# Expert layers of a macaron block: probability moved into the gated product, rows passed on summed in PSUM, token numbers as bfloat16 parts, scatters and gathers in pairs

## What is computed

```python
scores = softmax(xf @ gate_w.T)                  # 8192 x 64
_, idx = top_k(scores + gate_b, 6)               # six experts of each token
# the first 128 tokens that chose expert e fill its 128 slots, in order; later ones are dropped
h  = silu(xb[e] @ w1[e].T) * (xb[e] @ w3[e].T)   # 128 x 176 for each of 64 experts
yb = h @ w2[e].T                                 # 128 x 256
y[token of slot] += yb * scores[token, e]
z  = silu(xf @ ws1.T) * (xf @ ws3.T) @ ws2.T     # shared expert, all tokens
x  = x + 0.5 * (y + z)
```

## Time and profile before

| | us |
|---|---|
| median of three runs | 1974.1 |
| the profiled execution's own time | 1970.14 |
| its span in the trace | 1968.3 |
| PE busy | 1787.3 (91%) |
| DVE busy | 1337.4 (68%) |
| ACT busy | 1095.1 (56%) |
| POOL busy | 837.4 (43%) |

### The profile page before, as it was taken

The page is one execution under the profiler, slowest core; times in us unless marked ns, Lnnn a source line. Parts: engine busy times, 40 slices in busy tenths (PEclk is TensorE's granted clock), DMA queues, the critical chain, the costliest instruction groups (busy, mean ns, idle before and its releaser), DMA issues. The chain is left out here.

```text
span 1968.3 us, 31892 instructions
## 1 busy us (share of the span) xinstructions
PE 1787.3 (91%) x10553; PEld 1097.5 (56%) x10554; DVE 1337.4 (68%) x3338; ACT 1095.1 (56%) x2260; POOL 837.4 (43%) x923
## 2 busy tenths in 40 slices
PE   5999999899955889999999999999699999989997
PEld 2565656677732345444444444445356666657775
DVE  3787877566637567777777777767168787856664
ACT  3676776111113667777777777777466766731111
POOL 1010100687735665555555555550000111027777
PEclk9999999999978989999999999999899999999999
DMA  2233331799943333333333333332213343339997
GB/s 94 87 99 113 117 119 57 221 261 261 262 78 80 91 82 107 99 98 106 101 98 101 104 99 99 98 87 56 89 48 105 92 138 97 100 93 261 264 263 157
DMA packets 193342, 245.21 MB, mean 125 GB/s; under 512 B 17658, under 2 KB 160410, under 8 KB 193182
## 3 DMA queue, kind: packets, MB, share of 16 engines
q1 hardware_dynamic: 168606, 205.43, 34.4%
q0 software_dynamic: 24576, 37.77, 10.0%
HBM read 127.78 MB, written 63.86 MB: 97 GB/s over the span
## 5 line engine op out<-in xcount | busy, mean ns | idle before, releaser
L1332 DVE TENSOR_REDUCE a_smax<-a_p_ring 128x1 f32<-128x512 f32 (+2 forms) x768 | 353.7, 505 | 151.3 <-PE a_p_ring L1419 146.2
L1237 ACT ACTIVATE a_probs<-a_p_ring 128x512 f32<-128x512 f32 x640 | 363.8, 606 | 105.3 <-PE a_p_ring L1431 104.0
L1419 PE MATMUL a_p_ring<-p_ks,p_qs 100*128 100x512 bf16 (+3 forms) x1024 | 245.2, 304 | 43.1 <-ACT a_probs L1237 20.1
L48 POOL TENSOR_TENSOR f_rstd<-f_mv,eps 128x4 f32<-128x4 f32 x32 | 26.0, 813 | 552.9 <-DVE f_mv L42 548.4
L1431 PE MATMUL a_p_ring<-p_qs,p_ks 103*128 103x512 bf16 (+3 forms) x1024 | 243.2, 304 | 5.8 <-ACT a_probs L1237 5.4
L629 ACT ACTIVATE e_silu<-e_p_up 128x176 f32<-128x176 f32 x128 | 40.7, 318 | 353.6 <-PE e_p_up L719 226.4
L458 PE MATMUL f_p_up<-f_xnT,f_ws1T 128*128 128x512 f32 x384 | 187.9, 612 | 1.5 <-ACT f_xnT L253 1.5
L595 POOL DMA_INDIRECT e_got<-rows,slot_token x128 | 126.4, 988 | 141.5 <-issue 81.5
L499 PE MATMUL f_p_z<-f_ws2T,f_hidden 128*128 128x256 f32 (+1 forms) x768 | 184.5, 391 | 1.9 <-DVE f_hidden L346 1.9
L1447 PE MATMUL a_p_out<-a_probs,p_v 128*32 128x512 f32 (+3 forms) x2048 | 176.8, 445 | 6.2 <-ACT a_probs L1237 6.2
L458 PE MATMUL f_p_up<-f_xnT,f_ws3T 128*128 128x512 f32 x384 | 181.5, 595 | 0.0
(11 more groups left out here) (156 smaller groups left out, 3572.0 us busy)
## 6 DMA issues: line engine op xcount, KB each, us to landing
h_w<-w_in SPq DMA_DIRECT2D x128, 352.0 KB
p_qs<-a_parts SPq DMA_DIRECT2D x192, 128.0 KB, 2.4
p_ks<-a_parts SPq DMA_DIRECT2D x192, 128.0 KB, 2.5
h_w<-w_in SPq DMA_DIRECT2D x128, 176.0 KB
rows<-f_row SPq DMA_DIRECT2D x32, 640.0 KB, 6.3
h_x<-x_in SPq DMA_DIRECT2D x16, 512.0 KB, 6.0
acc<-h_x SPq DMA_DIRECT2D x16, 512.0 KB, 3.1
a_x<-acc SPq DMA_DIRECT2D x16, 512.0 KB, 4.0
```

What stands on the lines that cost most here:

```text
L1237: nc.scalar.activation(to[:], p_score[s][:], ACT.Exp, scale=SCALE).then_inc(score_free[s], 1)
L1332: ins = nc.vector.tensor_reduce(smax[:, t, 4 * g + h:4 * g + h + 1], p_score[s][:, at:at + length], AX.X, ALU.max)
L1419: ins = nc.tensor.matmul(p_score[s][:, at:at + length], qs[1 - u][0:SR + MASK, 4 * g + h, t * P:(t + 1) * P], ks[1 - u][0:SR + MASK, 4 * g ...
```

## The change

- Twelve lanes for the gathered rows instead of eight (`GOT`), with twelve gathers ahead; the lane counts on over both layers.
- On POOL the loop issues scatter e and e + 1, and after every odd one the next two gathers, instead of one gather ahead of each scatter.
- The probability is multiplied in by the instruction that multiplies the two halves on DVE; the factor 0.5 goes into ACT's copy of the turned product.
- The join matmul accumulates into `p_y` behind the w2 product; DVE then only copies `p_y` to `y`, and the second DVE instruction and its bank `p_join` are gone.
- The token numbers are split in two parts that bfloat16 holds exactly (tile times 128, and lane); `spread` does two bfloat16 matmuls for each expert instead of one in float32.
- `table` outlives the routing stage, `place` takes its folded content, and a bfloat16 identity is kept.

```diff
+GOT = 12
-        got = [sb(f"got{s}", [P, ROW]) for s in range(LANES)]
+        got = [sb(f"got{s}", [P, ROW]) for s in range(GOT)]
...
+        def lane(e):
+            return (to.first + e) % GOT
...
-                for e in range(LANES):
+                for e in range(GOT):
                     gather(e)
                 for u in range(XR):
                     pool.wait_ge(to.acc_stored[u], 16 * B // XR)
                 for e in range(E):
-                    pool.wait_ge(y_scaled, e + 1)
-                    if e + LANES < E:
-                        gather(e + LANES)
+                    pool.wait_ge(y_copied, e + 1)
                     wait_count(pool, added[e % 2], 16 * (e // 2))
                     if e % GROUP == 0:
                         pool.wait_ge(redirected, e // GROUP + 1)
                     add(e)
+                    if e % 2:
+                        for n in range(e - 1 + GOT, min(e + 1 + GOT, E)):
+                            gather(n)
...
-                    nc.scalar.copy(hiddenT[e % 2][:], p_hidden[:]).then_inc(hiddenT_ready, 1)
+                    nc.scalar.activation(hiddenT[e % 2][:], p_hidden[:], ACT.Copy, scale=0.5).then_inc(hiddenT_ready, 1)
...
-                    nc.vector.tensor_tensor(hidden[e % 2][:], silu[e % 2][:], p_up[e % 2][:, I:2 * I],
-                                            ALU.mult).then_inc(hidden_ready, 1)
-
-                def scale(e):
+                    nc.vector.scalar_tensor_tensor(hidden[e % 2][:], silu[e % 2][:], got[lane(e)][:, e + D:e + D + 1],
+                                                   p_up[e % 2][:, I:2 * I], ALU.mult,
+                                                   ALU.mult).then_inc(hidden_ready, 1)
+
+                def bring_y(e):
 
                     dve.wait_ge(y_ready, e + 1)
                     wait_count(dve, added[e % 2], 16 * (e // 2 - LANES // 2 + 1))
-                    ins = nc.vector.tensor_scalar(y[e % LANES][:], p_y[e % 2][:], got[e % LANES][:, e + D:e + D + 1],
-                                                  0.5, ALU.mult, ALU.mult)
-                    if e:
-                        dve.drain()
-                        ins = nc.vector.tensor_tensor(y[e % LANES][:], y[e % LANES][:], p_join[:], ALU.add)
-                    ins.then_inc(y_scaled, 1)
+                    nc.vector.tensor_copy(y[e % LANES][:], p_y[e % 2][:]).then_inc(y_copied, 1)
 
                 def tokens():
 
                     nc.vector.tensor_copy(token[:], w.slot_token[:])
+                    nc.vector.tensor_scalar(vacant[:], w.table[:, 1, :], 0.0, None, ALU.is_equal)
+                    nc.vector.tensor_scalar(tile_base[:], w.table[:, 1, :], float(P), float(-P), ALU.mult, ALU.add)
                     dve.drain()
+                    nc.vector.scalar_tensor_tensor(token_lane[:], vacant[:], w.lane[:, 0:1], w.table[:, 0, :],
+                                                   ALU.mult, ALU.add)
+                    nc.vector.scalar_tensor_tensor(token_tile[:], vacant[:], float(DUMMY + P), tile_base[:],
+                                                   ALU.mult, ALU.add)
...
                     for g in range(2):
                         ins = nc.tensor.matmul(p_y[e % 2][:], hiddenT[e % 2][:, g, :], w2[e % slots][:, g, :],
-                                               start=(g == 0), stop=(g == 1))
+                                               start=(g == 0), stop=(g == 1 and e == 0))
 
                     if e:
-                        pe.wait_ge(y_scaled, e)
+                        pe.wait_ge(y_copied, e)
                         if (e - 1) % GROUP == 0:
                             pe.wait_ge(redirected, (e - 1) // GROUP + 1)
-                        ins = nc.tensor.matmul(p_join[:], same[(e - 1) // GROUP % 2][:, (e - 1) % GROUP, :],
-                                               y[(e - 1) % LANES][:], start=True, stop=True)
+                        ins = nc.tensor.matmul(p_y[e % 2][:], same[(e - 1) // GROUP % 2][:, (e - 1) % GROUP, :],
+                                               y[(e - 1) % LANES][:], start=False, stop=True)
...
-                        ins = nc.tensor.matmul(p_tokens[:, k, :], token[:, after:after + 1].to_broadcast([P, P]),
-                                               w.ident[:], start=True, stop=True)
+                        nc.tensor.matmul(p_tokens[:, k, :], token_tile[:, after:after + 1].to_broadcast([P, P]),
+                                         w.ident16[:], start=True, stop=False)
+                        ins = nc.tensor.matmul(p_tokens[:, k, :], token_lane[:, after:after + 1].to_broadcast([P, P]),
+                                               w.ident16[:], start=False, stop=True)
```

More of the change, by code:

```diff
@@ L81, in open_arrivals @@
     arrivals.x_loaded = [ctx.enter_context(nc.semaphore(f"x_loaded{u}")) for u in range(XR)]
-    arrivals.gathered = [ctx.enter_context(nc.semaphore(f"gathered{s}")) for s in range(LANES)]
+    arrivals.gathered = [ctx.enter_context(nc.semaphore(f"gathered{s}")) for s in range(GOT)]
     arrivals.weights_loaded = [ctx.enter_context(nc.semaphore(f"weights_loaded{s}")) for s in range(LANES)]
@@ L90, in open_handover @@
     to.x_loaded, to.x_rounds = arrivals.x_loaded, layer * B // XR
-    to.gathered, to.gather_rounds = arrivals.gathered, layer * E // LANES
-    to.weights_loaded, to.first_load = arrivals.weights_loaded, layer * E
+    to.gathered = arrivals.gathered
+    to.weights_loaded, to.first = arrivals.weights_loaded, layer * E
     to.w13 = [ctx.enter_context(nc.sbuf_tensor(f"{tag}_w13_{s}", [P, DC, SI], F32))[:] for s in range(LANES)]
@@ L162, in route_and_share @@
         hidden = [sb(f"hidden{j}", [P, T]) for j in range(3)]
-        table = sb("table", [P, 2, E])
-        empty = sb("empty", [P, E])
+        table, empty, place = w.table, sb("empty", [P, E]), sb("place", [P, E])
         zero = sb("zero", [P, P], BF16)
@@ L431, in _ @@
                 nc.vector.tensor_scalar(empty[:], table[:, 1, :], 0.0, w.dummy_row[:, 0:1], ALU.is_equal, ALU.mult)
[L432 to L433 removed]
+                nc.vector.scalar_tensor_tensor(place[:], table[:, 1, :], float(P), table[:, 0, :], ALU.mult, ALU.add)
                 dve.drain()
[L435 removed]
+                nc.vector.scalar_tensor_tensor(w.slot_token[:], place[:], float(-P), empty[:],
                                                ALU.add, ALU.add)
@@ L595, in gather @@
                     nc.gpsimd.indirect_dma_start(
-                        out=got[e % LANES][:], out_offset=None, in_=dram.rows,
+                        out=got[lane(e)][:], out_offset=None, in_=dram.rows,
                         in_offset=bass.IndirectOffsetOnAxis(ap=w.slot_token[:, e:e + 1].bitcast(U32), axis=0),
-                    ).then_inc(gathered[e % LANES], 16)
+                    ).then_inc(gathered[lane(e)], 16)
                 def add(e):
@@ L698, in _ @@
                     if e:
-                        scale(e - 1)
+                        bring_y(e - 1)
                     if e % GROUP == 2 and e // GROUP + 1 < E // GROUP:
@@ L707, in turn @@
                 def turn(e):
-                    pe.wait_ge(gathered[e % LANES], 16 * (e // LANES) + 16 * to.gather_rounds + 16)
+                    pe.wait_ge(gathered[lane(e)], 16 * ((to.first + e) // GOT) + 16)
                     wait_count(pe, xT_ready, e)
                     for h in range(DC):
-                        ins = nc.tensor.transpose(p_turn[:, h, :], got[e % LANES][:, h * P:(h + 1) * P], w.ident[:])
+                        ins = nc.tensor.transpose(p_turn[:, h, :], got[lane(e)][:, h * P:(h + 1) * P], w.ident[:])
                     ins.then_inc(turned, 1)
```

15 lines of the change are left out of this document (8 added, 7 removed).

## The result

The changed kernel takes **1984.56 us** in the median of 13 runs (1979.7 to 1991.39), the kernel before in the same session 1974.52 (13 runs, 1971.23 to 1979.39). The ratio is 1.0049, with an interval of 1.0038 to 1.0060: slower by about 10 us, where 7.5 us of gain were forecast. The time lies above the stated range of 1955 to 1978 us, in the direction of the rival "Landings grow: slower".

What follows compares the result with a forecast made beforehand. POOL and the landing of its scatters were taken to set each expert stage's end, PE having slack. Gains of 2.9 us (second stage) and 4.6 (first) made 7.5, giving 1966.6 us at the median, range 1955 to 1978.

Steps and rivals of the forecast that it cites:

- Landings grow: slower: Rival, chance 0.15: paired scatters land later on full DMA engines; gain gone from 0.07 us a step, 1982 us at 0.15.
- By twos in the middle: POOL's paired scatters and gathers mid-stage: pace and waits kept, 4.77 us distance unchanged; bounds 0 to 4 us a stage, effects cancel.
- more weight traffic: Argument within the slower rival: a faster PE asks for weights 3% sooner on full DMA engines, which may lengthen landings.
- The rule on round robin: DMA engines alternate between queues with work, so a longer weight queue wouldn't delay scatters more; no time given.
- The end: Last twelve scatters of each stage run free of gathers at 2.225 us each: 2.9 us gained in the second, 3.3 first.
- the trace is slower by 0.6 us: Scatter landing in the tail: 2.9 us from issue in the trace against the skill's estimated 2.3; the trace decides.
- Twelve gathers ahead: Start of each stage on POOL: scatter 2 doesn't move in the second stage, comes 1.35 us sooner in the first.
- Lanes: DVE's reuse of y lanes: five microseconds of margin; if lost, PE slows to POOL's pace at no cost to the end.
- Token spread: Spread matmuls on PE in bfloat16: 6.1 us of PE saved a stage, 12.2 in all, counted at nothing at the end.
- POOL sets the end: Bound reading: POOL and the landing of its scatters set each expert stage's end; PE is slightly faster and has slack.
- Join, probability, tokens: PSUM join saves about 0.55 us of DVE an expert; probability priced zero, tokens 1 us a stage beside PE's gather wait.

Runs made afterwards that it cites:

- light loads: Changed kernel in pairs, and its alternating variant, with w2 loads of experts 8 to 63 cut to 16 of 88 partitions: 0.9996 and 0.9983 against the kernel before.
- eight-lane kernel: Changed kernel with eight lanes and POOL alternating, its bfloat16 spread, PSUM join and moved probability kept: 0.9985 on the first chip, 0.9996 on the second.

## Why the prediction was wrong

**"By twos in the middle" is the step that failed.** It kept the pace and the waits of alternation, because the distance from the end of a scatter to the start of the one that waits for it, 4.77 us, is the same in pairs. The distance is the same, to 0.05 us. What the step put at nothing, without a reason, is a part of that distance which a transfer can't use: the time from its landing to the start of the scatter that waits. It is 0.27 us in alternation and 0.77 in pairs, where the two waits stand side by side. A landing was free up to 6.11 us after its scatter's start and is now free up to 5.63, with landings of 5.7 to 6.0 in the mean. The bounds of 0 to 4 us a stage had no term for this; the measured cost is 12.7 us in the second stage and 13.1 in the first, where 2.7 of it belong to the mask rows.

**The rival "Landings grow: slower" had the direction and the price, but not the mechanism.** By it the gain is gone from 0.07 us a step; measured are 13.1 / 50 = 0.26 and 12.7 / 50 = 0.25. But the landings didn't grow. That its time came closest is in part luck. What it saw rightly is how thin the margin was: the earlier trace rows showed eight landings past the limit already, at a DMA share that the earlier trace rows showed as full. At such a place half a microsecond either way decides.

**The faster PE as a cause** ("more weight traffic", in the same rival) fell: with the old spread the pairs lose as much (1.0058), with the new one alternation does not. That weights take part in how late a transfer lands is what the light loads speak for, with the waits of pairs at 3.6 and 3.3 us instead of 11.8 and more; the pairs with all weights ran on another chip.

**The rule on round robin** in the Trainium skill, "DMA: Bandwidth & Descriptors", "Queues, rings and completion order", was let speak for the forecast. It tells how a DMA engine takes turns between queues, and nothing of the time between a landing and the instruction that waits for it, which is what the pairs changed. The runs don't contradict it; it was no argument against a slower outcome.

**"The end" was right in its sum.** In the second stage the tail took 24.4 us where 24.5 was worked out; in the first 28.2 where it was 30.2, or 30.9 with the wait of scatter 52. The gain that stands there, 3.0 and 5.3 us, is real and pays part of the loss. The step is 24.4 / 11 = 2.22 us as before. Its reading as 1.56 us of issue and 2.9 of landing was wrong, and the hint at the failed step lay in it:

```profile
1969.23 3.76 DMA out<-e_y,e_slot_to
1972.99 0.01 POOLq L619
1973.01 0.73 issue
1973.74 3.80 DMA out<-e_y,e_slot_to
```

The scatter lands 3.76 us after its start, 2.2 after the end of its issue, and the next starts 0.75 later. The 2.9 us are these two together. The Trainium skill's "Anatomy of one DMA — SWDGE (gpsimd) path", in "DMA: Bandwidth & Descriptors", from which 2.3 us for the DMA and a step of 1.93 were estimated, would have had a tail of 21.2. Counted from the end of issue, its 2.3 agrees with the 2.2 of this trace; what the estimated step lacked is the 0.75. So the prediction's "the trace is slower by 0.6 us" set the estimate for a transfer against a transfer and a reaction.

**"Twelve gathers ahead" was right where measured after**: scatter 2 starts 1779.36 - 1757.23 = 22.1 us after the first gather, before 1773.09 - 1751.51 = 21.6 (no change was forecast), and in the first stage 1.2 us sooner (1.35 forecast). What the step did not see is the standstill on other chips, which costs more than that: in its profiles y(0) is 3 to 5.5 us late in each stage.

**"Lanes"** said that the margin of five microseconds may go, and PE is then slowed to POOL's pace at no cost. It went: the scatters lag up to 20 to 23 us behind y where they lagged under 9. PE waits for gathers behind them (13.8 us), and the end is POOL's all the same.

**Token spread.** PE's pace was forecast at 3.05 us an expert and is 3.035 while PE is free. A group of four took 1832.11 - 1819.97 = 12.14 us, and eight products of the spread start within 0.39:

```profile
1819.97 0.22 PE L755 MATMUL e_p_tokens<-ident,e_token_tile 128*128 128x128 bf16 x1
...
1820.36 0.22 PE L757 MATMUL e_p_tokens<-ident,e_token_lane 128*128 128x128 bf16 x1
...
1832.11 0.22 PE L755 MATMUL e_p_tokens<-ident,e_token_tile 128*128 128x128 bf16 x1
```

It was counted at nothing at the end and gave 0.9982 and 0.9986 alone, 3 to 4 us of PE's 12. So "POOL sets the end" holds for most of it, not for all. Part of what comes through shows at the start: y(0) is 0.3 to 0.9 us earlier in each stage, which no step had counted, and in the kernel before POOL's loop starts by that.

**Join, probability, tokens** were counted at nothing. DVE's instructions in the second stage:

```profile
L661 DVE COPY e_y<-e_p_y 128x256 f32<-128x256 f32 x64 | 27.2, 424 | 40.7 <-PE e_p_y L746 38.3 <-DMA out<-e_y,e_slot_to 2.1 <-PE e_p_y L739 0.3
L653 DVE SCALAR_TENSOR_TENSOR e_hidden<-e_silu,e_got,e_p_up 128x176 f32<-128x176 f32 x64 | 25.3, 396 | 53.4 <-ACT e_silu L633 53.4
```

The copy is 424 ns where 418 was put, the product 0.06 us longer than before, inside its bounds and hidden. The eight-lane kernel, which has all of them and the spread, measures 0.9985 and 0.9996; the spread alone has 0.9982 and 0.9986. What is left for them is too small to be told from nothing.

**The sum again with measured terms.** Forecast -7.5. Start -1.2 and +0.5, tails -5.3 and -3.0, steps +25.8: 16.8 us for the profiled pair of executions, whose difference is 16.1. The medians differ by 10, since the execution of before lay below its median and that of after above.

**What stays open.** Why a scatter starts half a microsecond later behind a wait of its own is not explained here; that it does stands in every profile. Pairs in which the scatter carries the wait for the landing were not run, so it isn't shown that they would lose nothing. Nor were pairs with all weights on the second and third chips. The standstill's cause is open too. Which version is best depends on the chip: alternation with twelve lanes has 0.9972 on the first but 1.0008 and 1.0027 on the others, the kernel with eight lanes 0.9985 on the first and 0.9996, no difference, on the second. The latter and the bfloat16 spread alone (0.9982 and 0.9986, first chip only) are the versions that were never slower than the kernel before, by a margin as small as what can be measured.

## What to carry to other kernels

Where instructions on a full DMA system already wait a little for their transfers to land, equal distances don't mean equal waits. Read from the trace not only how long a transfer takes to land but also how long after the landing the waiting instruction starts, and look at which waits stand right ahead of it: two side by side cost 0.5 us more here than one, and a new order of issue can move a wait without anyone meaning to. Put the rearrangement in a kernel by itself before bundling it with gains that are sure, because here 26 us of steps swallowed the 9 us that start and tails gave. And repeat a result of some tenths of a per cent on another chip before it is believed.

## What the hardware showed unexpectedly

- A scatter on POOL that waits for an earlier one to land starts 0.27 us after the landing when it carries that wait itself, and 0.72 to 0.79 when the wait is an instruction of its own because a second wait stands beside it. At equal bytes, equal distance and equal mean landings, that moved the waits of a stage from 2 to 6 us up to 9 to 17 us. Leaving out four fifths of w2's bytes, on another chip, went with waits of 3.5 in pairs.
- With twelve indirect gathers in a row at the start of a stage, ACT and DVE stood idle for 2.7 to 4.6 us at a time on two of three chips, with PE's signal late; with eight gathers, on one of these two, they did not. The first y came 3 to 5.5 us later in each stage.
- An indirect gather of 128 rows costs POOL 0.95 us in an undisturbed row of gathers, 0.99 in alternation, and 1.02 and 0.98 in pairs; a scatter 1.59, or 1.62 and 1.58. The sum is nearly the same: 6.36 us for two of each in alternation and 6.40 in pairs, gaps included.
